# One state's input moved from GpSimd to the turned route in four of six scan passes, and ScalarE's half products spread out

## The chip, the cores and the metric

The kernel runs on one core of one Trainium2 chip. The metric is the time of one execution on the device, in microseconds (us).

## The reference

Eight images of 96 x 64 x 64 go through group normalisation, a selective-scan block (layer 0) and a linear-attention and feed-forward block (layer 1). The change touches the scan of layer 0 alone. Its core, cut from the reference:

```python
def step(h, inp):
    u_t, d_t, b_t, c_t = inp
    dA = jnp.exp(d_t[..., None] * A)
    h = dA * h + (d_t * u_t)[..., None] * b_t[:, :, None, :]
    y = jnp.einsum('bkdn,bkn->bkd', h, c_t)
    return (h, y)
_, ys = jax.lax.scan(step, h0, (u_l, d_l, B_l, C_l))
```

`h` has 4 directions x 192 channels x 16 states per image, and the scan runs over 4096 positions. `d_t` is the softplus of a projection, `u_t` the convolved input, `b_t` and `c_t` are rows that all channels share.

## The kernel before, in words

Per image the kernel runs four stages, and the changed one is `scan()` (from L931). The 4 x 192 channels are packed into six **passes** of 128 partitions, T = 0 to 5: T = 0 and 3 hold 128 channels in row order, T = 1 and 4 hold 128 channels in column order (their input and output are read and written with a stride), T = 2 and 5 hold the 64 channels that are left of two directions. Each pass walks four **chunks** of 1024 positions, and each chunk 16 **steps**, one for a state n. So there are 24 chunks and 384 steps an image, 3072 steps in all.

What a step needs, by engine:

- ScalarE (ACT) computes the decay, `exp(delta * a_neg)` (L1253), and after the scan copies the last column of the state to `carry` (L1188). It also does the softplus of the next chunk in step 3 (L1194, with a table load ahead and one behind), takes the finished sum y in step 5 (L1181), and copies delta in step 7 (L1202).
- VectorE (DVE) runs the recurrence as one scan instruction (L1328). In step 5 it also makes the next chunk's `du = delta * u` (L1295). For the scan of a turned state it first waits for `turned`, and in step 5 that wait stands ahead of L1295.
- GpSimd (POOL) multiplies the state with the row C, which SP has spread over 128 partitions by DMA (L1360).
- TensorE (PE) sums the weighted states of a chunk in PSUM by matmuls with the identity (L1110, `add_up`). The table `SUMS_AT` says in which step which state is summed: in step n mostly state n-5, in step 12 two of them (6 and 7), in step 4 the last one of the chunk before, followed by the old y (`add_y`, L1124 in column order and L1126 otherwise).

The scan's input is `du * B` with row B of state n, and the string `MADE` gives for each state who makes it:

- **d**, by DVE: PE spreads row B into PSUM by two bf16 matmuls (L1055), DVE multiplies it with du (L1315) and then scans.
- **b**, by POOL: SP spreads row B by DMA into `b_sb`, POOL multiplies (L1349) into the single buffer `dbu`, three steps ahead of the scan.
- **t**, turned: once a chunk PE transposes du, with the positions on partitions (`turn_du`, L1092, in step `DUT_AT`), and B's columns (`turn_b`, L1084). ACT copies these out (L1217 in step `DUT_OUT_AT`, L1208) and multiplies the turned du by B as a scale per partition, in two halves of four blocks (L1234, `times_b`); `TURN_AT` gives for each turned state the steps of its two halves, and a step that is larger than the state's number lies in the chunk before. PE then transposes the product back (`turn_back`, L1101), at the head of the state's own step.

The order of the work on each engine is that of the program, written out by these tables. PE and ACT begin the work of step n when the scan of step n-2 is done, since PSUM and decay buffers alternate between two:

```python
if made(g, n) != BY_POOL:
    pe.wait_ge(S["scanned"], g * NS + n - 1 + CREDIT)
    if made(g, n) == TURNED:
        turn_back(g, n)
    else:
        spread(T, at, pb[n % 2], n).then_inc(S["b_mm"], 1)
for m in SUMS_AT[n]:
    ...
if n == DUT_AT and following:
    turn_du(g + 1)
```

On PE, step n is thus: wait for scan n-2, turn back or spread state n, sum, and last the extra work of `PRE_AT` (step 2: the next chunk's projection for delta, L1067), `BT_AT` (8) or `DUT_AT`. On ACT it is: exp of n, extra work, half products, carry of n-1. Every POOL multiplication of a state waits for the `carried` of that state.

Of the kernel before, what the change touches and what calls it, by code (L numbers as in the profile page):

```python
# [60 lines left out]
B_AHEAD = 5  # L61
POOL_AHEAD = 3
BY_DVE, BY_POOL, TURNED = "dbt"
MADE = ("dtdbdttbdtdbdttb", "dtdbdttbdtdbdttb", "dtdbdtdbdtdbdtdb")
TURNS = ((slice(1, 16, 4), slice(6, 16, 8)),) * 2 + ((slice(1, 16, 4),),)
TURN_AT = ({1: (14, 15), 5: (0, 1), 6: (2, 4), 9: (6, 7), 13: (8, 9), 14: (10, 11)},) * 2 + \
    ({1: (13, 14), 5: (15, 1), 9: (4, 6), 13: (8, 10)},)
BLOCKS = 8
TRING = 2
PRE_AT, SOFTPLUS_AT, DU_AT, DELTA_AT = 2, 3, 5, 7  # L70
BT_AT, BT_OUT_AT, DUT_AT, DUT_OUT_AT = 8, 9, 11, 12
Y_AT = 5
CAB1_AT, SUM_AT, CAB2_AT, CA_AT, X2_AT = 8, 12, 18, 22, 25
FIRST = 2
# [38 lines left out]
def build(nc, x, weights, phase_weights, setup_weights, out, gate_dram, gn_dram):  # L113
# [157 lines left out]
    with ExitStack() as ctx:  # L271
# [659 lines left out]
        def scan():  # L931
# [31 lines left out]
            def made(g, n):  # L963

                return BY_DVE if (g, n) == (0, 1) else MADE[g // NSC % 3][n]

# [8 lines left out]
            def turned_columns(T):  # L975

                return MADE[T % 3].count(TURNED) * len(orders(T))

            def turned_states(T):

                return [n for few in TURNS[T % 3] for n in range(NS)[few]]

            def orders(T):

                return (0,) if T % 3 == 0 else (1,) if T % 3 == 1 else (0, 1)
# [11 lines left out]
            with nc.Block() as block:  # L997
# [49 lines left out]
                def _(pe):  # L1047
# [24 lines left out]
                    def turn_b(T, at, g):  # L1072
# [4 lines left out]
                        for j in range(BLOCKS):  # L1077
                            block_cols = parts[own, 2 * (T // 3), span(at * SC + j * 128, 128)]
                            to = 16 * j
                            for few in TURNS[T % 3]:  # L1080
                                states = sel[own, few, first:first + 128 * count:128]
# [83 lines left out]
                def _(act):  # L1165
# [73 lines left out]
                    def turned_products(T, g, at_step, ahead):  # L1239

                        for n, halves in TURN_AT[T % 3].items():
                            for half, when in enumerate(halves):
# [714 lines left out]
```

## Time and profile before

| | us |
|---|---|
| median of three runs | 12057.92 (12057.77 to 12058.58) |
| the profiled execution | 12077.47 |
| its span in the trace | 12075.7 |

| engine | busy us | share of the span |
|---|---|---|
| PE | 10533.0 | 87% |
| VectorE | 10508.8 | 87% |
| GpSimd | 9499.6 | 79% |
| ScalarE | 9340.1 | 77% |

The profiled execution is some 20 us above the median. The shares are means over all stages; within the scan they are higher, and the windows of single passes show them.

### The profile page before, as it was taken

To read this page: it belongs to the slowest core of one execution; us is meant where nothing else is said; L and a number is where in the kernel's file an instruction comes from. 1 tells how busy PE (TensorE), PEld (TensorE's weight loads), DVE (VectorE), ACT (ScalarE), POOL (GpSimd) and SP (SyncE) were. 2 spreads that over 40 slices of the span, in tenths; PEclk is the share of its full clock that TensorE was granted. 3 is DMA by queue.
4 is the path that set the end of the run, shared out by engine and by line. 5 is a ranking of instruction groups with operands and counts; after the bars stand their busy time and mean duration, and the time that the engine had idled before them with its cause. 6 is when DMAs were issued, how large, how long until landed. Compare 5 with 4: busy or idle time off the path is not lost. (4 is left out here: it accounts for less than half of the span.)

```text
span 12075.7 us, 124888 instructions
## 1 busy us (share of the span) xinstructions
PE 10533.0 (87%) x35584; PEld 4912.7 (41%) x35584; DVE 10508.8 (87%) x7561; ACT 9340.1 (77%) x20418; POOL 9499.6 (79%) x4213
## 2 busy tenths in 40 slices
PE   7988889888898988989889898898988889888888
PEld 3444334443344433444334443344433444334443
DVE  7999779996799967999679996799967999679996
ACT  6888578885788857888578885788857888578885
POOL 5999459994599945999469993699936999369993
PEclk9999989999899999999999999899999999999999
DMA  4777447774477744777447773477735777357773
GB/s 142 223 223 221 107 135 223 223 221 105 136 223 222 222 102 141 222 225 222 97 145 226 223 221 92 150 223 223 220 90 154 222 222 223 86 160 220 224 221 78
DMA packets 673215, 2191.42 MB, mean 181 GB/s; under 512 B 160400, under 2 KB 162448, under 8 KB 661968
## 3 DMA queue, kind: packets, MB, share of 16 engines
q1 hardware_dynamic: 672528, 2183.44, 62.5%
q8 instruction: 287, 4.70, 0.2%
q14 instruction: 400, 3.28, 0.1%
HBM read 2085.75 MB, written 67.44 MB: 178 GB/s over the span
## 5 line engine op out<-in xcount | busy, mean ns | idle before, releaser
L1360 POOL TENSOR_TENSOR state<-state,c_sb 128x1024 f32<-128x1024 f32 x3072 | 7179.3, 2378 | 242.2 <-DMA c_sb<-bc 141.1
L1110 PE MATMUL ps<-state,wt 128*128 128x512 f32 x12288 | 5732.9, 599 | 62.8 <-ACT ya L1181 26.0
L1328 DVE TENSOR_TENSOR_SCAN state<-decay,carry,ps 128x1024 f32<-128x1024 f32 x1728 | 3987.7, 2337 | 41.9 <-issue 6.1
L1110 PEld LDWEIGHTS ps<-state,wt 128*128 128x128 f32 x12288 | 2263.0, 191 | 2252.1 <-issue 1927.2
L1234 ACT ACTIVATE dbu_t<-du_t,b_t 128x128 f32<-128x128 f32 (+1 forms) x10176 | 2951.1, 366 | 25.3 <-PE ps L1101 25.3
L1253 ACT ACTIVATE decay<-delta,a_neg 128x1024 f32<-128x1024 f32 x2304 | 2640.9, 1146 | 0.0
L1349 POOL TENSOR_TENSOR dbu<-b_sb,du 128x1024 f32<-128x1024 f32 x768 | 1820.1, 2370 | 176.2 <-DVE du L1333 153.7
L1315 DVE TENSOR_TENSOR ps<-ps,du 128x1024 f32<-128x1024 f32 x1288 | 1555.0, 1207 | 39.9 <-PE ps L1055 39.7
L1188 ACT COPY carry<-state 128x1 f32<-128x1 f32 x3072 | 568.3, 185 | 1277.8 <-DVE state L1328 1262.8
L1055 PE MATMUL ps<-parts,sel 114*128 114x512 bf16 (+1 forms) x2576 | 793.9, 391 | 817.3 <-DVE state L1328 816.7
L1328 DVE TENSOR_TENSOR_SCAN state<-ps,carry,dbu 128x1024 f32<-128x1024 f32 x576 | 1347.8, 2340 | 132.1 <-POOL dbu L1349 113.6
L1328 DVE TENSOR_TENSOR_SCAN state<-decay,ps 128x1024 f32<-128x1024 f32 x576 | 1296.6, 2278 | 16.2 <-PE ps L1101 4.8
L1101 PE MATMUL ps<-wt,dbu_t 128*128 128x128 f32 x8128 | 1093.6, 278 | 153.8 <-DVE state L1328 152.7
L1101 PEld LDWEIGHTS ps<-wt,dbu_t 128*128 128x128 f32 x8128 | 938.8, 142 | 645.2 <-DVE state L1328 322.3
L1253 ACT ACTIVATE ps<-delta,a_neg 128x1024 f32<-128x1024 f32 x768 | 853.1, 1111 | 0.0
L1055 PEld LDWEIGHTS ps<-parts,sel 114*128 114x128 bf16 (+1 forms) x2576 | 169.4, 97 | 1657.2 <-DVE state L1328 1520.6
L1676 POOL CAST h<-h16b 128x1536 fp8e5<-128x1536 f16 x64 | 113.2, 1768 | 919.5 <-DVE h16b L1800 919.5
L304 ACT ACT_TABLE_LOAD x409 | 524.7, 1283 | 66.5 <-DMA x_tok<-x 19.8
L1328 DVE TENSOR_TENSOR_SCAN state<-ps,dbu 128x1024 f32<-128x1024 f32 x192 | 437.6, 2279 | 62.3 <-POOL dbu L1349 59.7
L1662 POOL TENSOR_TENSOR sqa<-sqa,sqr 64x512 f32<-64x512 f32 x64 | 101.0, 1577 | 402.8 <-ACT sqr L1568 402.8
L534 ACT ACTIVATE rs<-ps,wt 96x512 f32<-96x512 f32 (+1 forms) x256 | 175.2, 684 | 308.2 <-PE ps L519 165.8
L1067 PE MATMUL ps<-parts,dt_w 114*128 114x512 bf16 (+1 forms) x1536 | 380.9, 392 | 29.9 <-PEq L696 29.9
(227 smaller groups left out, 9905.3 us busy)
## 6 DMA issues: line engine op xcount, KB each, us to landing
c_sb<-bc SPq DMA_DIRECT2D x2048, 512.0 KB, 4.6
c_sb<-bc SPq DMA_DIRECT2D x2048, 256.0 KB, 6.0
b_sb<-bc SPq DMA_DIRECT2D x512, 512.0 KB, 4.0
b_sb<-bc SPq DMA_DIRECT2D x512, 256.0 KB, 4.0
gates<-gate_a SPq DMA_DIRECT2D x8, 2048.0 KB, 6.8
x_tok<-x SPq DMA_DIRECT2D x256, 48.0 KB, 1.9
gn<-gn_t SPq DMA_DIRECT2D x8, 1536.0 KB, 7.1
gate_a<-gates SPq DMA_DIRECT2D x8, 1536.0 KB, 10.8
```

The source lines that it names most:

```text
L304: act.add_instruction(mybir.InstLoadActFuncSet(name=nc.get_next_instruction_name(), act_func_set_id=which, ins=[], outs=[]))
L1055: mm = pe.matmul(bank[:, q * CH:(q + 1) * CH], sel[own, n, first:first + 128], part_cols(at, 2 * (T // 3), q, own), start=True, stop=True)
L1067: mm = pe.matmul(pc[:, q * CH:(q + 1) * CH], dt_w[own, p, w, :], part_cols(at, k, q, own), start=(i == 0 and p == 0), stop=(i == len(ways) ...
L1101: mm = pe.transpose(pb[n % 2][:, j * 128:(j + 1) * 128], src[:, j, :], col("ident"))
L1110: mm = pe.matmul(py[:, q * CH:(q + 1) * CH], col("ident"), state[:, slot(g, n), q * CH:(q + 1) * CH], start=(n == 0), stop=False)
L1188: act.copy(carry[:, n:n + 1], state[:, slot(g, n), last:last + 1]).then_inc(S["carried"], 1)
L1234: last = act.activation(dbu_t[turn % TRING][:, j, part], du_t[:, j, part], ACT.Copy, scale=b_t[:, g % 2, j, i:i + 1])
L1253: act.activation(pb[n % 2][:, :] if made(g, n) == BY_POOL else decay[:, n % 2, :], delta[:, g % 2, :], ACT.Exp, scale=a_neg[:, T, n:n + 1] ...
L1315: dve.tensor_tensor(pb[n % 2][:, :], pb[n % 2][:, :], du[:, g % 2, :], ALU.mult)\
L1328: dve.tensor_tensor_scan(state[:, slot(g, n), way], rate, what, 0.0 if fresh else carry[:, n:n + 1], ALU.mult, ALU.add)\
L1349: pool.tensor_tensor(dbu[:, :], b_sb[:, :], du[:, g % 2, :], ALU.mult)\
L1360: pool.tensor_tensor(state[:, slot(g, n), :], state[:, slot(g, n), :], c_sb[:, n % CRING, :], ALU.mult).then_inc(S["weighted"], 1)
```

## The change

In the passes T = 0, 1, 3 and 4 the order of the makers becomes `dtdtdtdbtdtbtdtb` where it was `dtdbdttbdtdbdttb`. Six states stay with DVE, seven are turned (1, 3, 5, 8, 10, 12 and 14) instead of six, and three are POOL's (7, 11 and 15) instead of four. No two turned states stand next to each other. `TURNS` lists the turned states for `turn_b`, and `TURN_AT` gives ACT one half product in each of 14 steps, all but 3 and 5. In T = 2 and 5 the makers stay, and the halves of states 1 and 5 come a step later. In all passes du is turned in step 12 instead of 11 and copied out in step 14 instead of 12.

```diff
-MADE = ("dtdbdttbdtdbdttb", "dtdbdttbdtdbdttb", "dtdbdtdbdtdbdtdb")
+MADE = ("dtdtdtdbtdtbtdtb", "dtdtdtdbtdtbtdtb", "dtdbdtdbdtdbdtdb")
...
-TURN_AT = ({1: (14, 15), 5: (0, 1), 6: (2, 4), 9: (6, 7), 13: (8, 9), 14: (10, 11)},) * 2 + \
-    ({1: (13, 14), 5: (15, 1), 9: (4, 6), 13: (8, 10)},)
+TURN_AT = ({1: (14, 15), 3: (0, 1), 5: (2, 4), 8: (6, 7), 10: (8, 9), 12: (10, 11), 14: (12, 13)},) * 2 + \
+    ({1: (14, 15), 5: (0, 1), 9: (4, 6), 13: (8, 10)},)
...
-BT_AT, BT_OUT_AT, DUT_AT, DUT_OUT_AT = 8, 9, 11, 12
+BT_AT, BT_OUT_AT, DUT_AT, DUT_OUT_AT = 8, 9, 12, 14
```

TensorE around step 12 of a chunk of T = 0, before. The rows are the turning back of state 9, sum of 3, spread of 10, sums of 4 and 5, turning of du, spread of 12, sums of 6 and 7, turning back of 13, sum of 8:

```order
L1101 MATMUL ps<-wt,dbu_t_117 128x128 x8
L1110 MATMUL ps<-state,wt 128x512 x2
L1055 MATMUL ps<-parts,sel 128x512 x2
L1110 MATMUL ps<-state,wt 128x512 x4
L1092 MATMUL ps<-wt,du 128x128 x8
L1055 MATMUL ps<-parts,sel 128x512 x2
L1110 MATMUL ps<-state,wt 128x512 x4
L1101 MATMUL ps<-wt,dbu_t_116 128x128 x8
L1110 MATMUL ps<-state,wt 128x512 x2
```

The same place in the changed kernel: turning back of 10, sums of 4 and 5, turning back of 12, sums of 6 and 7, turning of du, spread of 13, sum of 8, turning back of 14:

```order
L1101 MATMUL ps<-wt,dbu_t_117 128x128 x8
L1110 MATMUL ps<-state,wt 128x512 x4
L1101 MATMUL ps<-wt,dbu_t_116 128x128 x8
L1110 MATMUL ps<-state,wt 128x512 x4
L1092 MATMUL ps<-wt,du 128x128 x8
L1055 MATMUL ps<-parts,sel 128x512 x2
L1110 MATMUL ps<-state,wt 128x512 x2
L1101 MATMUL ps<-wt,dbu_t_117 128x128 x8
```

Between the wait for scan 10 and the next spread there now stand a turning back, two sums and the turning of du; before, the turning of du stood ahead of that wait and the spread right behind it.

TensorE in steps 2 to 5 of a column pass (T = 1), before: spread of 2, sum, projection, sum (step 3), spread of 4, sum, the old y by L1124, turning back of 5:

```order
L1055 MATMUL ps<-parts,sel 128x512 x2
L1110 MATMUL ps<-state,wt 128x512 x2
L1067 MATMUL ps<-parts,dt_w 128x512 x6
L1110 MATMUL ps<-state,wt 128x512 x2
L1055 MATMUL ps<-parts,sel 128x512 x2
L1110 MATMUL ps<-state,wt 128x512 x2
L1124 MATMUL ps<-ya,wt 128x512 x2
L1101 MATMUL ps<-wt,dbu_t_117 128x128 x8
```

And in the changed kernel:

```order
L1055 MATMUL ps<-parts,sel 128x512 x2
L1110 MATMUL ps<-state,wt 128x512 x2
L1067 MATMUL ps<-parts,dt_w 128x512 x6
L1101 MATMUL ps<-wt,dbu_t_116 128x128 x8
L1110 MATMUL ps<-state,wt 128x512 x2
L1055 MATMUL ps<-parts,sel 128x512 x2
L1110 MATMUL ps<-state,wt 128x512 x2
L1124 MATMUL ps<-ya,wt 128x512 x2
L1101 MATMUL ps<-wt,dbu_t_117 128x128 x8
```

The turning back of state 3 is new, ahead of the sum of step 3.

ScalarE in steps 10 to 12 of a chunk of the changed kernel: exp of 10, first half of 12, carry of 9, exp of 11, second half of 12, carry of 10, exp of 12:

```order
L1253 ACTIVATE decay<-delta,a_neg 128x1024
L1234 ACTIVATE dbu_t_116<-du_t,b_t 128x128 x4
L1188 COPY carry<-state 128x1
L1253 ACTIVATE ps<-delta,a_neg 128x1024
L1234 ACTIVATE dbu_t_116<-du_t,b_t 128x128 x4
L1188 COPY carry<-state 128x1
L1253 ACTIVATE decay<-delta,a_neg 128x1024
```

The second half of state 12 stands behind the carry of state 9, in the step before the one in which TensorE turns state 12 back.

## Rows read from the trace of the kernel before

**Rows 1.** The page, busy time of the engines, share of the span:
```profile
PE 10533.0 (87%) x35584; PEld 4912.7 (41%) x35584; DVE 10508.8 (87%) x7561; ACT 9340.1 (77%) x20418; POOL 9499.6 (79%) x4213
```

**Rows 2.** Windows, third image, T 0-4: length; busy PE, PEld, DVE, ACT, POOL; clock; DMA:
```profile
3200.40:3384.10 183.70, 166.07 (x613) 78.77 (x614) 179.50 (x93) 158.95 (x352) 177.38 (x77) 0.95 0.69 222
3384.10:3570.80 186.70, 169.98 (x632) 83.25 (x631) 179.71 (x94) 161.97 (x361) 186.70 (x82) 1.00 0.67 227
3570.80:3764.20 193.40, 168.82 (x579) 79.25 (x579) 187.45 (x100) 162.42 (x401) 184.30 (x80) 0.98 0.91 217
3764.20:3949.80 185.60, 164.30 (x634) 82.36 (x633) 178.72 (x93) 158.00 (x349) 185.60 (x81) 1.00 0.68 227
3949.80:4136.60 186.80, 169.93 (x631) 83.21 (x631) 179.89 (x93) 161.91 (x361) 186.80 (x82) 1.00 0.67 225
```

**Rows 3.** Timeline of POOL, second chunk of T = 3 (start, us, instructions merged):
```profile
3839.47 2.36 POOL L1349 TENSOR_TENSOR dbu<-b_sb,du 128x1024 f32<-128x1024 f32 x1
3841.79 9.32 POOL L1360 TENSOR_TENSOR state<-state,c_sb 128x1024 f32<-128x1024 f32 x4
3851.07 2.35 POOL L1349 TENSOR_TENSOR dbu<-b_sb,du 128x1024 f32<-128x1024 f32 x1
```

**Rows 4.** Timeline of DVE, same chunk, steps 10 to 15:
```profile
3838.28 1.21 DVE L1315 TENSOR_TENSOR ps<-ps,du 128x1024 f32<-128x1024 f32 x1
3839.52 2.35 DVE L1328 TENSOR_TENSOR_SCAN state<-decay,carry,ps 128x1024 f32<-128x1024 f32 x1
3841.87 2.35 DVE L1328 TENSOR_TENSOR_SCAN state<-ps,carry,dbu 128x1024 f32<-128x1024 f32 x1
3844.13 1.21 DVE L1315 TENSOR_TENSOR ps<-ps,du 128x1024 f32<-128x1024 f32 x1
3845.38 6.82 DVE L1328 TENSOR_TENSOR_SCAN state<-decay,carry,ps 128x1024 f32<-128x1024 f32 x3
3853.46 2.35 DVE L1328 TENSOR_TENSOR_SCAN state<-ps,carry,dbu 128x1024 f32<-128x1024 f32 x1 [1.26 <-POOL dbu L1349]
```

**Rows 5.** Timeline of PE, same chunk, steps 11 to 13:
```profile
3840.06 1.05 PE L1092 MATMUL ps<-wt,du 128*128 128x128 f32 x8
3841.92 0.61 PE L1055 MATMUL ps<-parts,sel 114*128 114x512 bf16 x2 [0.82 <-DVE state L1328]
3842.37 3.60 PE L1110 MATMUL ps<-state,wt 128*128 128x512 f32 x8
3845.80 1.05 PE L1101 MATMUL ps<-wt,dbu_t 128*128 128x128 f32 x8
3846.69 1.88 PE L1110 MATMUL ps<-state,wt 128*128 128x512 f32 x4
```

**Rows 6.** Timeline of ACT, same chunk, carry of 12 and the half product of step 14:
```profile
3847.76 0.19 ACT L1188 COPY carry<-state 128x1 f32<-128x1 f32 x1 [2.27 <-DVE state L1328]
...
3848.91 1.26 ACT L1234 ACTIVATE dbu_t<-du_t,b_t 128x128 f32<-128x128 f32 x4
```

**Rows 7.** Timeline of PE, second chunk of T = 1, steps 3 to 5:
```profile
3436.26 1.88 PE L1110 MATMUL ps<-state,wt 128*128 128x512 f32 x4
3438.54 0.61 PE L1055 MATMUL ps<-parts,sel 114*128 114x512 bf16 x2 [0.41 <-DVE state L1328]
3438.99 1.88 PE L1110 MATMUL ps<-state,wt 128*128 128x512 f32 x4
3440.70 3.59 PE L1124 MATMUL ps<-ya,wt 128*128 128x512 f32 x4
3444.12 1.95 PE L1101 MATMUL ps<-wt,dbu_t 128*128 128x128 f32 x16
```

**Rows 8.** Timeline of DVE, same chunk, du in step 5:
```profile
3445.22 1.97 DVE L1295 TENSOR_TENSOR du<-ps,ua 128x1024 f32<-128x1024 f32 x1 [0.86 <-PE ps L1101]
```

**Rows 9.** Waits of the whole span: us in total, times, longest:
```profile
POOL state L1360 <- DMA c_sb<-bc: 141.1, 200, 2.6
...
DVE du L1295 <- PE ps L1101: 73.7, 64, 1.9
```

More of the change, by code:

```diff
@@ L63 @@
 BY_DVE, BY_POOL, TURNED = "dbt"
-MADE = ("dtdbdttbdtdbdttb", "dtdbdttbdtdbdttb", "dtdbdtdbdtdbdtdb")
-TURNS = ((slice(1, 16, 4), slice(6, 16, 8)),) * 2 + ((slice(1, 16, 4),),)
-TURN_AT = ({1: (14, 15), 5: (0, 1), 6: (2, 4), 9: (6, 7), 13: (8, 9), 14: (10, 11)},) * 2 + \
-    ({1: (13, 14), 5: (15, 1), 9: (4, 6), 13: (8, 10)},)
+MADE = ("dtdtdtdbtdtbtdtb", "dtdtdtdbtdtbtdtb", "dtdbdtdbdtdbdtdb")
+TURNS = ((slice(1, 6, 2), slice(8, 16, 2)),) * 2 + ((slice(1, 16, 4),),)
+TURN_AT = ({1: (14, 15), 3: (0, 1), 5: (2, 4), 8: (6, 7), 10: (8, 9), 12: (10, 11), 14: (12, 13)},) * 2 + \
+    ({1: (14, 15), 5: (0, 1), 9: (4, 6), 13: (8, 10)},)
 BLOCKS = 8
```

## The prediction

> **What bounds the kernel now.** The page comes first: PE and VectorE are both busy for 87% of the span and POOL for 79% [rows 1]. These are means over four stages, so the windows of single passes come next. In T = 1, 3 and 4 POOL is busy for the whole window (186.7 of 186.7 us, 185.6 of 185.6, 186.8 of 186.8), while DVE has 7 us to spare in each, PE 17 to 21 and ACT 25 to 28 [rows 2]. In T = 2 nobody is at the window's length: POOL has 184.3 of 193.4 us and DVE 187.5, with DMA at 0.91 [rows 2]. POOL's timeline shows the cycle of the POOL-bound passes: one product and four weighted states take 3851.07 - 3839.47 = 11.60 us, 2.32 an instruction, 46.4 us a chunk of 20 [rows 3]. On DVE this shows as a wait of 1.26 us for `dbu` in step 15 [rows 4]. So POOL is the clock of four passes out of six, and taking an instruction from it does reach the end, up to the next limit.
>
> **POOL after.** 19 instructions a chunk, 19 x 2.32 = 44.1 us. The removed product and its spread row B (one DMA of 512 KB) are the whole saving there.
>
> **DVE after.** A scan costs 2.26 us (3844.13 - 3841.87), a product 1.24 (3839.52 - 3838.28) [rows 4]. Sixteen scans and six products are 36.16 + 7.44 = 43.6; DVE's busy time in T = 3, 178.7 / 4 = 44.7, leaves 1.1 for du, and du read with a stride costs 1.97 instead [rows 2, 8], 0.8 more. The number of DVE's instructions doesn't change, so with no waits a chunk takes 44.7, or 45.5 with the stride. DVE takes over from POOL as the clock. By passes: T = 3 (one strided du) 179.7; T = 0 the same plus 1.24, since state 1 of the first chunk is always a DVE product, 180.9; T = 1 and 4 (three strided) 181.2. Before they took 185.6, 183.7, 186.7 and 186.8 [rows 2]. That is what the change can win; now the waits that it adds on DVE's path.
>
> **Step 13, the main term.** State 13 is now a DVE product, and its row B is spread by PE behind all of PE's step 12. Let 0 be the end of scan 10. PE's step 12 needs both that scan and the second half product of state 12, which ACT makes in step 11, behind the carry of scan 9. Scan 9 ends at -2.26; the carry starts 0.1 later (scan 12 of rows 4, carry of rows 6), the half product 1.15 after the carry starts and ends 1.26 later [rows 6]: +0.25. PE starts 0.05 after what it waits for (3841.92 against the scan's end at 3841.87) [rows 4, 5], so at 0.30. Then come the turning back, 0.89 (3846.69 - 3845.80), two sums, 3.43 (3845.80 - 3842.37), the turning of du, eight matmuls like the first, 0.89, and the spread with 0.61 to its end [rows 5], and 0.05 to the product: 6.17. DVE is through with scans 11 and 12 at 2 x 2.26 - 0.09 = 4.43. **The product of state 13 is 1.74 us late**, in each chunk of four passes. Nothing behind wins it back, since DVE is the clock. Before, the same place had no wait: the turning of du stood ahead of the wait for scan 10, under PE's idle time of 0.82, and the turning back of 13 was needed only at the scan [rows 5]. A pass pays 4 x 1.74 = 7.0.
>
> **Step 5 in column order.** There the old y costs PE 3.42 (3444.12 - 3440.70), and `du` waited 0.86 for the turning back of 5 behind it [rows 7, 8]. It now also stands behind the turning back of state 3. Before, PE was free at 3436.26 + 1.71 = 3437.97 and waited until 3438.54 [rows 7]; of the new 0.89 these 0.57 hide all but 0.32. With the 0.09 by which instructions overlap, the wait becomes 0.95 + 0.32 = 1.3 in the second and third chunk. In the fourth the projection for T = 2 has twelve matmuls, there was no idle time to hide in, and its wait lies between the mean 73.7 / 64 = 1.15 and the longest, 1.9 [rows 9]; I take 1.75, near the longest as the longer projection says, plus 0.89: 2.65. A column pass pays 1.3 + 1.3 + 2.65 = 5.3. It paid some of this before as well, but hidden, because POOL was later still.
>
> **Costed at nothing.** The seventh turned state adds 8 transposes (0.89) to PE, which has 17 us of 187 to spare, and two half products, 2.5 us a chunk, to ACT: 40.5 + 2.5 = 43.0 of 45 [rows 2]. Both are covered but for the places above; ACT's halves are one a step, and an exp is due only after the scan that runs beside it. Step 9 (spread behind one sum and `turn_b`) and step 3 (behind the projection) I followed in the same way, and PE arrives 0.7 and 0.9 us early. The later copy of du (step 14) falls in the pause that step 13 makes. `b_sb` and `c_sb` have more time than before.
>
> **T = 2 and 5.** The makers stay. PE's step 12 now holds the turning of du ahead of the turning back of 13: 0.05 + 0.45 + 3.43 + 0.89 + 1.05 + 0.05 = 5.9 against a scan due at 5.7, 0.2 late, but there DVE waits for POOL anyway, and POOL for rows C (141.1 us in all) [rows 9]. POOL enters these passes less behind than before, by at most the product it no longer has plus some, 2.7 us. Bounds: 2.7 less, 2.1 more (0.2 a chunk, and as much again from the later halves and a longer wait in step 5). I take 1 us less a pass, since POOL's backlog builds up again within two chunks.
>
> **Sum**, an image: T = 0: 180.9 + 7.0 - 183.7 = +4.2; T = 1: 181.2 + 7.0 + 5.3 - 186.7 = +6.8; T = 3: 179.7 + 7.0 - 185.6 = +1.1; T = 4: +6.7; T = 2 and 5: -2. Together +16.8, less 0.4 for rounding in the column passes' waits, 16.4 x 8 = **+131 us**. The profiled execution would take 12077.5 + 131 = 12,208, and the median, which lies 20 lower, 12057.9 + 131 = **12,190 us**.
>
> **The rivals.**
>
> *Every wait stays hidden, the bound is simply the next busiest engine.* Then the four passes fall to DVE's busy time, by 4.2 + 7.0 + 6.9 + 6.9 = 25.0 an image [rows 2]: 200 us, 11,858. For it speaks that all engines stay below the window; against it that DVE already waited for PE in step 5 [rows 8]. The Trainium skill ("Perfetto Trace Analysis", Identifying the Most-Contended Engine) ranks engines by occupancy and says to optimise the highest first; by that rule this change is right and this would be the outcome. The trace agrees that POOL was the highest in these passes, but not that DVE runs without waits once it is next. Chance 0.04.
>
> *Step 13 is not late* (the other side of my forecast): PE's step 12 would have to be through within 4.43 us of the end of scan 10, for instance by ACT's half being early and PE's eight transposes overlapping the sums more than their rows say. It decides at 1.74 us of PE work. It gives 7.0 x 4 x 8 = 223 us less, 11,967. Against it: the five pieces are rows, in program order on one engine. Chance 0.09.
>
> *The change doesn't shift the clock*: POOL still sets 46.4 us a chunk, waiting for carries that ACT, now fuller, delivers late, while products vanish. Then 12,058, no difference. POOL had no idle time that would show such waits [rows 2]. Chance 0.07.
>
> *TensorE's clock falls with more transposes.* The granted clock was 1.00 in T = 1, 3 and 4 with six turned states a chunk, and 0.98 in T = 2 with four, so more turning went with the higher of the two levels, 2.4 GHz [rows 2]. If the four passes ran at the 0.95 of the first window, 5% of 743 us an image, 37 us, would come on top: 12,190 + 297 = 12,487. Chance 0.03. The Trainium skill ("TensorE: Matmul & The Clock Gate", Part 4: PE-mode transpose) says that transposes don't count as busy for the clock, which speaks against this change; this case's rows don't bear it out.
>
> **How the numbers follow.** The forecast has 0.77. Its own range: step 13 from 1.4 (ACT's half in time) to 2.0 us, -43 to +33; T = 2 and 5 from -27 to +33; step 5 by 10: 12,120 to 12,245. The full range goes down to 12,050 to take in the case of no change, and leaves out the two faster cases and the clock, 0.16. A measurement of this kernel tells about 0.2%, 24 us, from no change. Faster 0.13 (the first two rivals), same 0.07, slower 0.80.
>
> **What would show it.** In the new profile POOL is busy for less than its window in T = 1, 3 and 4. In T = 0, 1, 3, 4 DVE's L1315 waits for PE's L1055 once a chunk, about 1.7 us, some 128 times and 220 us in all, where it had practically no such wait; the wait of L1295 for L1101 grows in column order; waits for `dbu` vanish there. A pass T = 1 lasts about 193.5 us and T = 3 about 186.7. I am wrong if L1315 doesn't wait, if T = 1 is shorter than 186 us, or if ACT's carries hold POOL.

## The result and the profile after

| | before | changed |
|---|---|---|
| median, us | 12058.25 (12057.77 to 12061.76) | 12262.88 (12255.01 to 12268.58) |
| profiled execution, us | 12077.47 | 12263.92 |

The changed kernel is slower by 204.6 us. The ratio is 1.0169, with a 95% interval of 1.0151 to 1.0186. I had forecast 12,190, slower by 131, with a range up to 12,245: the direction is right, and the result lies above the range. The two profiled executions differ by 186 us of span, the medians by 205; what follows accounts for the 186, since only they have a trace. The medians in this document are of runs in the chip's usual state: one of the four runs of the kernel with the sums ahead took 13,745 us at a mean granted clock of 0.739 and is left out.

The page after, to be held against [rows 1], the engines' busy time:

```profile
PE 10764.3 (88%) x36608; PEld 5091.3 (42%) x36608; DVE 10499.5 (86%) x7561; ACT 9631.9 (79%) x21442; POOL 9226.6 (75%) x4085
```

128 POOL instructions and 273 us of its work are gone, 1024 matmuls and 1024 activations have come. VectorE does the same work, 7561 instructions. The windows of the passes T = 0 to 4 of the third image (length; busy PE, PEld, DVE, ACT, POOL; clock; DMA), to be held against [rows 2]:

```profile
3237.50:3429.70 192.20, 173.51 (x645) 83.96 (x646) 179.48 (x94) 168.31 (x384) 175.09 (x76) 0.92 0.64 207
3429.70:3624.30 194.60, 176.06 (x663) 87.99 (x663) 179.72 (x93) 170.64 (x390) 176.20 (x76) 0.98 0.63 206
3624.30:3816.40 192.10, 167.58 (x579) 78.29 (x578) 187.09 (x100) 162.79 (x405) 182.40 (x80) 0.99 0.90 214
3816.40:4006.30 189.90, 172.78 (x666) 88.24 (x665) 178.06 (x93) 167.25 (x381) 180.82 (x79) 0.96 0.63 216
4006.30:4204.00 197.70, 180.38 (x663) 89.81 (x663) 179.91 (x92) 170.88 (x389) 176.77 (x76) 0.96 0.61 203
```

POOL is no longer busy for the whole window in any pass. DVE's busy time hasn't moved (179.7 against 179.7 in T = 1), and yet the passes are longer: in T = 1 DVE now stands still for 15 us of 194.6. The granted clock has fallen in the passes T = 1, 3 and 4, where it was 1.00, to 0.98, 0.96 and 0.96.

The waits of the whole span name the engine that DVE stands still for (us in total, times, longest):

```profile
DVE ps L1315 <- PE ps L1055: 361.8, 226, 5.0
...
DVE du L1295 <- PE ps L1101: 118.5, 88, 2.3
```

The second was 73.7 before, 64 times [rows 9]. The first was, before:

```profile
DVE ps L1315 <- PE ps L1055: 39.7, 8, 5.0
```

So the product L1315 waits for the spread L1055, 322 us more. It does so 226 times: the 8 of before, once in each of the 128 chunks, as I had expected, and 90 times more. A timeline of one chunk (first of T = 4) shows both places. PE from step 6 to the spread of step 13:

```profile
4020.36 3.70 PE L1110 MATMUL ps<-state,wt 128*128 128x512 f32 x8
4027.39 1.23 PE L1101 MATMUL ps<-wt,dbu_t 128*128 128x128 f32 x8 [3.33 <-DVE state L1328]
4028.41 3.49 PE L1110 MATMUL ps<-state,wt 128*128 128x512 f32 x4
4031.74 0.57 PE L1084 MATMUL ps<-sel,parts 114*128 114x3 bf16 x16
4032.16 0.59 PE L1055 MATMUL ps<-parts,sel 114*128 114x512 bf16 x2
...
4038.94 1.07 PE L1101 MATMUL ps<-wt,dbu_t 128*128 128x128 f32 x8 [0.15 <-ACT dbu_t L1234]
4039.85 3.59 PE L1110 MATMUL ps<-state,wt 128*128 128x512 f32 x8
4043.28 1.05 PE L1092 MATMUL ps<-wt,du 128*128 128x128 f32 x8
4044.17 0.59 PE L1055 MATMUL ps<-parts,sel 114*128 114x512 bf16 x2
```

DVE in the same chunk, step 8 to step 13:

```profile
4029.43 2.26 DVE L1328 TENSOR_TENSOR_SCAN state<-decay,ps 128x1024 f32<-128x1024 f32 x1
4032.79 1.23 DVE L1315 TENSOR_TENSOR ps<-ps,du 128x1024 f32<-128x1024 f32 x1 [1.10 <-PE ps L1055]
4034.06 4.46 DVE L1328 TENSOR_TENSOR_SCAN state<-decay,ps 128x1024 f32<-128x1024 f32 x2
4038.44 2.27 DVE L1328 TENSOR_TENSOR_SCAN state<-ps,dbu 128x1024 f32<-128x1024 f32 x1
4040.62 2.26 DVE L1328 TENSOR_TENSOR_SCAN state<-decay,ps 128x1024 f32<-128x1024 f32 x1
4044.80 1.23 DVE L1315 TENSOR_TENSOR ps<-ps,du 128x1024 f32<-128x1024 f32 x1 [1.92 <-PE ps L1055]
```

The second wait, in step 13, is the forecast one, piece by piece. PE's step 12 starts 0.42 us after the end of scan 10 (4038.94 - 4038.52; two scans in 4.46 from 4034.06), released by ACT's half product; then 0.91, 3.43, 0.89 and 0.59, and DVE's product starts at 4044.80, 6.28 us after scan 10. I had 6.17.

The first, in step 9, was in no term. PE sums states 0 and 1, then has nothing to do for 3.33 us, until scan 6 is done. When it resumes, one sum takes 3.49 us for four matmul records, where [rows 5] has 1.88: it runs at about half speed. Before, the idle time ahead of step 8 was at most 1.9 us in any chunk of these passes; in the first chunk of T = 1:

```profile
3404.22 0.60 PE L1055 MATMUL ps<-parts,sel 114*128 114x512 bf16 x2 [1.71 <-DVE state L1328]
```

Back in the chunk of T = 4 of the changed kernel, the windows just before, in and behind the idle time show the granted clock (the column before the last two):

```profile
4020.00:4023.70 3.70, 3.70 (x10) 1.44 (x8) 3.70 (x2) 2.62 (x7) 3.70 (x3) 1.00 0.30 101
4023.70:4027.40 3.70, 0.37 (x2) 0.02 (x1) 3.67 (x4) 3.36 (x8) 3.70 (x2) 1.00 0.82 257
4027.50:4031.20 3.70, 3.70 (x12) 2.06 (x13) 3.70 (x2) 3.41 (x8) 3.70 (x3) 0.60 0.92 283
```

The clock was at the upper level (2.4 GHz) before and in the idle stretch, and at the lower (1.2 GHz) for most of the 3.7 us after it. PE's step 8 (turning back, sum, `turn_b`) lasts 1.7 us longer, and the spread for state 9 comes that much later.

The clock fell like this in 90 of the 128 chunks, and those are the 90 in which the product of state 9 waits; in the other 38 it doesn't wait. The length of the idle stretch alone doesn't decide it. Of the 38 chunks that kept the clock, 30 had an idle stretch of 2.2 to 3.3 us, and of those that lost it some had only 2.2. The third and the last chunk of T = 1, third image, show one of each:

```profile
3548.66 1.10 PE L1101 MATMUL ps<-wt,dbu_t 128*128 128x128 f32 x8 [2.94 <-DVE state L1328]
3597.77 1.66 PE L1101 MATMUL ps<-wt,dbu_t 128*128 128x128 f32 x8 [2.21 <-DVE state L1328]
```

In the 3.7 us from there the first has a granted clock of 1.00 and the second 0.55. What else decides it isn't known.

### The profile page after: what moved, and what is told of

Read it like the earlier page. It is cut to its first block and busy times, and to the rows that moved or that the text cites. A ratio compares the mean times of both kernels' runs of the same rounds, so it can differ in the third digit from the quotient of the medians.

```text
span 12262.1 us, 127832 instructions
## 1 busy us (share of the span) xinstructions
PE 10764.3 (88%) x36608; PEld 5091.3 (42%) x36608; DVE 10499.5 (86%) x7561; ACT 9631.9 (79%) x21442; POOL 9226.6 (75%) x4085
## 3 DMA queue, kind: packets, MB, share of 16 engines
q14 instruction: 406, 3.33, 0.1%
## 5 line engine op out<-in xcount | busy, mean ns | idle before, releaser
L1110 PE MATMUL ps<-state,wt 128*128 128x512 f32 x12288 | 5837.1, 609 | 109.5 <-ACT ya L1181 46.1
L1328 DVE TENSOR_TENSOR_SCAN state<-decay,carry,ps 128x1024 f32<-128x1024 f32 x1824 | 4222.7, 2337 | 42.3 <-PE ps L1101 5.9
L1234 ACT ACTIVATE dbu_t<-du_t,b_t 128x128 f32<-128x128 f32 (+1 forms) x11200 | 3276.4, 368 | 15.1
L1253 ACT ACTIVATE decay<-delta,a_neg 128x1024 f32<-128x1024 f32 x2432 | 2788.1, 1146 | 0.0
L1315 DVE TENSOR_TENSOR ps<-ps,du 128x1024 f32<-128x1024 f32 x1288 | 1560.8, 1212 | 361.8 <-PE ps L1055 361.8
L1101 PE MATMUL ps<-wt,dbu_t 128*128 128x128 f32 x9152 | 1285.4, 285 | 426.8 <-DVE state L1328 363.0
L1101 PEld LDWEIGHTS ps<-wt,dbu_t 128*128 128x128 f32 x9152 | 1089.3, 146 | 1100.1 <-DVE state L1328 762.6
L1349 POOL TENSOR_TENSOR dbu<-b_sb,du 128x1024 f32<-128x1024 f32 x640 | 1513.7, 2365 | 0.0
L1328 DVE TENSOR_TENSOR_SCAN state<-decay,ps 128x1024 f32<-128x1024 f32 x608 | 1371.8, 2277 | 15.9 <-PE ps L1101 4.5
L1055 PE MATMUL ps<-parts,sel 114*128 114x512 bf16 (+1 forms) x2576 | 794.1, 391 | 452.5 <-DVE state L1328 449.2
L1328 DVE TENSOR_TENSOR_SCAN state<-ps,carry,dbu 128x1024 f32<-128x1024 f32 x480 | 1117.4, 2328 | 22.7 <-POOL dbu L1349 20.8
L1253 ACT ACTIVATE ps<-delta,a_neg 128x1024 f32<-128x1024 f32 x640 | 711.4, 1112 | 0.0
L1055 PEld LDWEIGHTS ps<-parts,sel 114*128 114x128 bf16 (+1 forms) x2576 | 182.0, 97 | 1100.6 <-DVE state L1328 973.9
```

Of the source, the lines that this page charges most:

```text
L1055: mm = pe.matmul(bank[:, q * CH:(q + 1) * CH], sel[own, n, first:first + 128], part_cols(at, 2 * (T // 3), q, own), start=True, stop=True)
L1101: mm = pe.transpose(pb[n % 2][:, j * 128:(j + 1) * 128], src[:, j, :], col("ident"))
L1110: mm = pe.matmul(py[:, q * CH:(q + 1) * CH], col("ident"), state[:, slot(g, n), q * CH:(q + 1) * CH], start=(n == 0), stop=False)
L1234: last = act.activation(dbu_t[turn % TRING][:, j, part], du_t[:, j, part], ACT.Copy, scale=b_t[:, g % 2, j, i:i + 1])
L1253: act.activation(pb[n % 2][:, :] if made(g, n) == BY_POOL else decay[:, n % 2, :], delta[:, g % 2, :], ACT.Exp, scale=a_neg[:, T, n:n + 1] ...
L1315: dve.tensor_tensor(pb[n % 2][:, :], pb[n % 2][:, :], du[:, g % 2, :], ALU.mult)\
```

## The experiments

Each kernel was run with kernels before on the same chip; there the kernel before had medians of 12,066 to 12,071, some 10 us more than in the table above. The changed kernel itself wasn't run there again, so a difference from its 12,262.9 is uncertain by those 10 us; the ratios to before are not. Four questions: are the two waits separate, is the clock the cause of the one in step 9, how is the step 13 term composed, and what is the change worth without them.

**Du turned in step 11 again**, on the changed kernel:

```diff
-BT_AT, BT_OUT_AT, DUT_AT, DUT_OUT_AT = 8, 9, 12, 14
+BT_AT, BT_OUT_AT, DUT_AT, DUT_OUT_AT = 8, 9, 11, 14
```

> The changed kernel with the turning of du back in step 11. Theory A (two separate waits: the product of state 13 waits for what TensorE does in step 12, the product of state 9 for TensorE at half clock): the step 13 wait falls by the 0.89 us of eight transposes, 1.83 to 0.94 us, 128 times, so about 114 us less than the changed kernel, 12,263 - 114 = 12,150; the wait of step 9 stays near 0.8 us and the granted clock near 0.953. Theory B (one cause, the clock; step 13 is late because TensorE never recovers): moving the transposes changes the time by under 30 us, 12,235 or more.

Measured 12,186.4, 76 us less than the changed kernel; ratio to before 1.0096 (1.0081 to 1.0111). Neither number of the expectation is met exactly, 12,150 was 36 too low, and the gain is well above the rival's 30. The step 13 wait fell in the column pass as forecast; DVE in the second chunk of T = 1:

```profile
3494.08 1.23 DVE L1315 TENSOR_TENSOR ps<-ps,du 128x1024 f32<-128x1024 f32 x1 [0.86 <-PE ps L1055]
```

The total of this wait is 267.4 us, 94 less: 71 of them in step 13 (231 to 160) and 23 in step 9 (91 to 68), where the clock now falls in 69 chunks instead of 90. So the step 9 wait stayed for the most part, with the clock at 0.957. In T = 3 and 4, from the second chunk on, step 13 waits 0.85 us where the clock has held in step 8 and 1.33 where it has fallen; in T = 0 it waits up to 1.6.

**The idle stretch cut in two.** In step 7 PE has no turning back or spread, so nothing kept the sum of state 1 from following that of state 0. One wait moves it to the middle of the idle time:

```diff
+if n == 7 and T % 3 < 2:
+    pe.wait_ge(S["scanned"], g * NS + n - 1 + CREDIT)
 if made(g, n) != BY_POOL:
     pe.wait_ge(S["scanned"], g * NS + n - 1 + CREDIT)
```

> The changed kernel with one wait more: in the passes with seven turned states TensorE holds the sum of step 7 until scan 5 is done, so that its 3.4 us of idle time ahead of step 8 is cut into two shorter ones; its work and its order stay. Theory A (the clock falls after that idle stretch, and the half-speed matmuls of step 8 make the product of state 9 late): the granted clock comes back to about 0.965, the step 9 wait of about 0.8 us (12.6 us an image) goes, the time falls by about 100 us to 12,163. Rival (TensorE simply has too much to do in steps 8 and 9): an added wait can't help, the time stays at 12,263 or rises.

Measured 12,167.6, 95 us less than the changed kernel (ratio to before 1.0078, 1.0061 to 1.0095), clock 0.968. An added wait made the kernel faster. PE in the same chunk (first of T = 4; the two lines more in the file shift L1315 to L1317):

```profile
3984.04 1.98 PE L1110 MATMUL ps<-state,wt 128*128 128x512 f32 x4
3987.63 1.98 PE L1110 MATMUL ps<-state,wt 128*128 128x512 f32 x4 [1.60 <-DVE state L1330]
3991.08 1.10 PE L1101 MATMUL ps<-wt,dbu_t 128*128 128x128 f32 x8 [1.46 <-DVE state L1330]
3992.02 1.88 PE L1110 MATMUL ps<-state,wt 128*128 128x512 f32 x4
```

The idle time is now 1.60 and 1.46 us, the sum behind it takes 1.88 again. The passes T = 1, 3 and 4 have the clock at 1.00, the last for instance, 5.2 us shorter than in the changed kernel:

```profile
3970.00:4162.50 192.50, 173.79 (x663) 85.89 (x663) 179.45 (x92) 170.41 (x389) 177.26 (x77) 1.00 0.62 208
```

and DVE's waits for the spread are now one a chunk, beside the 8 of before:

```profile
DVE ps L1317 <- PE ps L1055: 270.8, 136, 5.0
```

That is the clean number for the step 13 wait: (270.8 - 39.7) / 128 = 1.81 us. The profile counts it from the end of scan 12; against the start that the forecast took, 0.09 earlier, the product is 1.90 late. The clock as cause of the step 9 wait is shown: same work, same order, only the place of the idle time differs, and in step 8 the clock is at 1.00 in all 128 chunks.

**Both together**:

> Both edits, the turning of du in step 11 and the split idle time. Theory A: the gains add, 114 + 100 us, to about 12,050, the time before. If the step 13 wait were a consequence of the clock the two would not add, and the result would lie near that of the split alone.

Measured 12,067.3, ratio 0.9998 (0.9989 to 1.0007): the time before. The two gains were 76 and 95 alone, and are 196 together, so they don't just add: with the clock steady the earlier turning of du brings 100 us (12,167.6 - 12,067.3), and DVE's waits for the spread are 104 us shorter in all than with the split alone:

```profile
DVE ps L1317 <- PE ps L1055: 166.9, 136, 5.0
```

In the first run part of that was lost to the clock: step 13 waited 160 us there in all and 127 here.

**The old makers with the new steps** (du turned in step 12 and copied out in 14, halves of T = 2 and 5 later):

> The kernel before, with only the step numbers of the change: du turned in step 12 and copied out in step 14, and the half products of T = 2 and 5 a step later; makers and turned states as before. Theory A (the turning of du hurts only where a DVE product follows in step 13, and VectorE has time to spare while GpSimd is the clock): within 15 us of before, 12,058. Rival (the later turning of du is at fault by itself): slower by the 0.89 us a chunk, some 100 us or more.

Measured 12,083.4, ratio 1.0010 (1.0001 to 1.0020): 13 us more than before on the same chip, within the 15 of the theory. The later turning of du isn't free even so: T = 0 takes 3.2 us an image more, with a wait of the scan of state 13 for its turning back in every chunk, and T = 2 and 5 take 3.1 less together, so that two effects cancel in the total. In T = 1, 3 and 4, where POOL is the clock, it costs 0.1, 0.1 and 1.0 us an image. The rival's 100 us are far off: the large loss needs a DVE product behind the turning of du.

**ScalarE's halves of 8, 10, 12 and 14 one step earlier**:

```diff
-8: (6, 7), 10: (8, 9), 12: (10, 11), 14: (12, 13)
+8: (5, 6), 10: (7, 8), 12: (9, 10), 14: (11, 12)
```

> The changed kernel with ScalarE's half products of states 8, 10, 12 and 14 one step earlier each (steps 5 to 12). It tests the one piece of the step 13 term that isn't TensorE's own: the second half of state 12 ends 0.3 to 0.4 us after scan 10. Theory A: TensorE's step 12 starts at the end of scan 10, the step 13 wait falls by about 0.35 us, 128 times, 45 us: about 12,218. Rival: ScalarE's half is never what TensorE waits for, the time stays at 12,263.

Measured 12,217.5, 45 us less than the changed kernel; ratio to before 1.0128 (1.0113 to 1.0143). PE and DVE in the second chunk of T = 1, where step 12 now starts on the end of scan 10 and not on ACT:

```profile
3496.48 1.10 PE L1101 MATMUL ps<-wt,dbu_t 128*128 128x128 f32 x8 [0.50 <-DVE state L1328]
...
3502.38 1.23 DVE L1315 TENSOR_TENSOR ps<-ps,du 128x1024 f32<-128x1024 f32 x1 [1.47 <-PE ps L1055]
```

The wait in that chunk was 0.27 us longer in the changed kernel. 0.27 x 128 = 35 us come from there. The waits in step 9 are 19 us shorter in all, with a clock of 0.957 instead of 0.953; the expectation had nothing of this, so the agreement of the total with my 45 is partly luck.

**The sums one step earlier**, on the changed kernel, which takes one of the two sums out of step 12 and puts one into the idle stretch:

```diff
-(0,), (1,), (2,), (3,), (4,), (5,), (6, 7), (8,), (9,), (10,))
+(0,), (1, 2), (3,), (4,), (5,), (6,), (7,), (8,), (9,), (10,))
```

> The changed kernel with the sums of states 2 to 7 one step earlier: states 1 and 2 in step 7, then one a step, so that step 12 has a single sum and step 7 fills TensorE's idle stretch with work. Theory A: step 12 is 1.71 us shorter, 0.41 + 0.89 + 1.71 + 0.89 + 0.60 = 4.5 us against the 4.43 in which VectorE is through, so the step 13 wait falls from 1.83 to about 0.1 us (220 us less), the idle stretch ahead of step 8 to under 2 us, so the clock holds and the step 9 wait goes as well (100 us less): about 11,940. Rival: the sums, moved forward, wait for GpSimd's weighted states and block TensorE there; then the time stays above 12,100.

Measured 11,970.2 (the middle one of three runs), ratio to before 0.9927 (0.9908 to 0.9947), clock 0.969: 293 us less than the changed kernel, and faster than before. Expected were 320. DVE's wait for the spread is 51.3 us in all, so 0.09 us a chunk are left beside the 39.7 of before. The idle stretch is 1.22 us, and POOL's weighted states are there in time:

```profile
3416.28 1.10 PE L1101 MATMUL ps<-wt,dbu_t 128*128 128x128 f32 x8 [1.22 <-DVE state L1328]
3417.22 1.88 PE L1110 MATMUL ps<-state,wt 128*128 128x512 f32 x4
```

**And du turned in step 11**:

> The sums ahead as in the run before, and du turned in step 11. Theory A: step 13 was nearly free of a wait already, so this gains at most 0.1 us a chunk, 15 us, against the sums alone: 11,925. If the turning of du cost its 0.89 us wherever it stands, it would gain some 100 us.

Measured 11,966.8, ratio 0.9921 (0.9906 to 0.9936), 3 us less than without, and 10 less in the profiled executions; both lie within the spread of the runs (11,953 to 11,986). The eight transposes that were worth 100 us in the run with both edits are worth at most 10 here, because there is hardly a product waiting behind them any more.

**And the old y out of the way of state 5** (the last sums of the old chunk one step earlier, so that state 15's falls in step 3; its old y is added alone in step 4, no longer straight behind that sum; the preparation of the next chunk is in step 1; du stays turned in step 11):

```diff
-PRE_AT, SOFTPLUS_AT, DU_AT, DELTA_AT = 2, 3, 5, 7
+PRE_AT, SOFTPLUS_AT, DU_AT, DELTA_AT = 1, 3, 5, 7
...
-SUMS_AT = ((11,), (12,), (13,), (14,), (15,), (), (0,),
+SUMS_AT = ((11,), (12,), (13, 14), (15,), (), (), (0,),
...
+if n == 4 and previous:
+    add_y(previous[0], chunk_at(*previous)).then_inc(S["y_summed"], 1)
```

> The run before with the projection for delta in step 1, the sums of states 14 and 15 one step earlier, and the old y still added in step 4: this takes 1.3 + 1.7 us of TensorE's work out of the way of the turning back of state 5 in column order. Theory A: the wait of L1295 in step 5 falls from 1.3 to about 0.3 us in the column chunks, and the longer ones of T = 1 and 4 (2.3) and of T = 2 and 5 (1.9) by about 1 each, some 60 us in all: 11,865. Rival: the sums of 14 and 15 then wait for GpSimd, and nothing is gained.

Measured 11,909.4, ratio to before 0.9871 (0.9856 to 0.9886), 57 us less than the run before, where 60 were expected; the 11,865 was taken from an expected start 42 us too low. It is the fastest of all kernels here, 1.3% under the kernel before. The waits (a line shift of one) have come down to:

```profile
DVE du L1296 <- PE ps L1101: 35.0, 70, 0.7
```

from 105.9 in the run before and 118.5 in the changed kernel. T = 1 of the third image takes 182.4 us, with DVE busy for 179.18 of them:

```profile
3336.70:3519.10 182.40, 172.35 (x664) 86.58 (x663) 179.18 (x92) 169.49 (x386) 176.70 (x77) 1.00 0.66 218
```

DVE is the clock of this pass, as the change had it in view.

**The same order of TensorE with the old makers.** This tells whether the moved state matters at all, or only the order:

> TensorE's new order (sums ahead, old y late, du turned in step 11) with the makers of the kernel before: six turned states and four of GpSimd's. Theory A: GpSimd is the clock with 20 instructions a chunk, 46.4 us, and its order is untouched, so TensorE's order wins nothing by itself: 12,040 to 12,066, at most 10 us from the fourth chunks of the column passes. Rival (the gain of the last runs is TensorE's order alone and the moved state brings nothing): near 11,909.

Measured 12,070.2, ratio 1.0000 (0.9991 to 1.0009), 4 us above the expected range and even with before on the same chip (12,069.1). TensorE's order alone brings nothing; its T = 1 of the third image is POOL's from end to end:

```profile
3379.80:3565.20 185.40, 170.77 (x631) 82.73 (x631) 179.68 (x93) 162.58 (x361) 185.40 (x81) 1.00 0.69 226
```

So the moved state, with ScalarE's steps that belong to it, is worth some 160 us (12,070.2 - 11,909.4, on two chips whose kernels before differ by 3) when TensorE delivers in time. Either part alone gains nothing: the order brings 0, the moved state in the old order of sums costs 205.

**The halves of T = 2 and 5 alone**, on the kernel before:

```diff
-({1: (13, 14), 5: (15, 1), 9: (4, 6), 13: (8, 10)},)
+({1: (14, 15), 5: (0, 1), 9: (4, 6), 13: (8, 10)},)
```

> The kernel before with one line of the change: in T = 2 and 5 the half products of states 1 and 5 one step later. It is to tell where the 5.8 us an image come from that these passes got shorter by. Theory C (the later halves themselves let ScalarE's exp and carries come earlier): T = 2 and 5 shorter by 2 to 3 us an image together, 20 us in all, 12,046. Rival D (they got shorter because GpSimd enters them with less backlog, or its transfers land sooner): no difference, 12,066.

Measured 12,071.2, ratio 1.0002 (0.9993 to 1.0011); T = 2 and 5 took 0.5 and 1.1 us an image more than in the trace of before. The later halves aren't why T = 2 and 5 became shorter.

## Why the prediction was wrong, point by point

The measured change by passes, the mean over eight images from the first scan of a pass to that of the next (of T = 5 to the end of its last scan), in us an image: T = 0 +8.6 (forecast +4.2), T = 1 +8.5 (+6.8), T = 2 -3.2 (-1), T = 3 +3.6 (+1.1), T = 4 +8.3 (+6.7), T = 5 -2.5 (-1). Together, before rounding, 23.4 x 8 = 187 against 131.

- **POOL after, DVE the next clock.** Right. No pass with the new makers is POOL's.
- **DVE's time without waits** was taken 1.5 us a pass too high, 6.0 an image in the four passes. Most of it stood in the rows: the 44.7 a chunk is the mean of T = 3, which holds one strided du already, and I put the stride on top once more. DVE's busy times in [rows 2] are 179.5, 179.7, 178.7 and 179.9 where I had 180.9, 181.2, 179.7 and 181.2, 5.2 us an image less.
- **Step 13, the main term.** Right in mechanism, and near in size: the product is 1.90 us late against 1.74, 2.8 us an image more in all. The surplus is ACT's part: PE's step 12 starts 0.42 us after scan 10 where I had 0.30, and that part is confirmed by the run that took it away.
- **Step 5 in column order.** Right: waits of 1.3 us in the second and third chunk and of 2.3 in the fourth, which with the 0.09 of overlap are 1.4, 1.4 and 2.4 where I had 1.3, 1.3 and 2.65. The wait also appeared in T = 0, up to 0.46 us, 1.6 us an image with the overlap, where I had left it out: before, the turning back of 5 was done only 0.1 to 0.6 us ahead of `du` there in three of the four chunks, and the new 0.89 used that up.
- **The step that failed** is "costed at nothing: PE arrives 0.7 us early" in step 9. It took TensorE's speed from rows at the full clock. In the changed order PE runs out of work in step 7 for 3.3 us, and the clock falls behind it in 90 of 128 chunks. The product of state 9 comes 12.5 us an image later by it, 100 us in all; the run with the split idle stretch gives 95 us back. That is more than the 56 us that the sum missed, since other terms, too high by some 44 together, cancelled part of it. With the idle stretch split the kernel takes 12,167.6, inside my range; that the miss looked small, 18 us beyond the range, is luck.
- **The clock rival** had the right resource and the wrong mechanism. I had asked whether more transposes lower the clock, found that the rows say no, and gave it 0.03. The question to ask was which idle stretch gets longer. With the order printed ahead of the prediction it could have been answered: before, step 6 was a turned state, with more for PE to do than the spread that stands there now (eight transposes in 0.89 us against 0.45), and DVE's step 6 was a scan alone, 2.26 us; now it is a product and a scan, 3.5 us, so scan 6, for which PE waits at the head of step 8, comes 1.24 us later, and step 7 holds only a sum. The Trainium skill ("TensorE: Matmul & The Clock Gate", Part 1) says that TensorE is throttled to 1.2 GHz by default and that activity releases it. This case's trace agrees: 0.60 of full speed in the 3.7 us behind 3.33 us of idle time, and 1.00 with idle times of 1.60 and 1.46.
- **T = 2 and 5** came out 5.7 us an image shorter, where I had 2. My bound of 2.7 a pass was just exceeded by one and held the other. That they shorten wherever the passes before them aren't POOL's (48.1 us a chunk in T = 2 with du in step 11, 48.0 with both edits, 48.8 with the old makers) speaks for GpSimd's smaller backlog, and the last run rules out the later halves by themselves; the backlog itself wasn't tested alone, and the old makers with the new steps had 48.3, which it doesn't explain. That run shortened T = 2 and 5 by 3.1 us an image, more than half of the 5.7, and beside the halves it differs from before only in the steps in which du is turned and copied out. Why they shorten stays open.

The sum with the measured terms, an image: 16.4 forecast, +12.5 (step 9), +2.8 (step 13), +1.6 (step 5 in T = 0), -0.2 (step 5 in column order), -6.0 (DVE's time without waits, which is what the waits leave of the passes), -3.7 (T = 2 and 5) = 23.4. Since the sixth term is such a remainder, that the sum comes out is no proof of the single terms.

Of the other rivals, that of the next busiest engine gives the best view of what was possible: it asked for 200 us less than before, and the kernel with all places mended takes 157 less. Occupancy named the right engine to relieve; it said nothing on the two places where the relieved engine's work then arrived late.

## What to carry to other kernels

When work is moved from the engine that is the clock, walk the other engines' program order once a step with the new clock's spacing: a free share of 9% on TensorE didn't prevent up to two waits per chunk, because what counts is how much stands between a wait and the instruction that the clock engine needs. Look in the same walk for the longest stretch in which TensorE has nothing to do, not only for where it is late; if it grows, the work behind it may run at half speed, and spreading the same work over the gap (a sum earlier, even an added wait) cost nothing here. A change that loses by such a wait may still be right: here the same table of makers is 1.7% slower in one order of TensorE and 1.3% faster in another.

## What the runs showed of the hardware that was not expected

- Behind an idle stretch of 3.33 us, in an engine that is busy for some 90% of these passes, the granted clock fell; four matmul records then took 3.49 us instead of 1.88. It fell at this place in 90 of 128 chunks, behind idle stretches of 2.2 to 3.6 us, and held in 30 chunks with stretches of 2.2 to 3.3.
- A wait put into TensorE's program made the kernel 95 us faster, by cutting 3.33 us of idle time into 1.60 and 1.46.
- In the first chunk of a pass, where the scans begin from zero instead of a carry, they follow each other every 2.18 to 2.20 us instead of 2.26 (4029.43 - 4027.25 is such a pair in the changed kernel).
